# A graph layer on one Trainium2 core: a destination block normalized in its own turn and recorded in three turns instead of six

## The chip, the cores and the metric

The kernel runs on one NeuronCore of a Trainium2 chip. The metric is device time in microseconds (us). Each engine of the core (TensorE or PE, VectorE or DVE, ScalarE or ACT, GpSimd or POOL, SyncE or SP) runs its own stream of instructions in order and waits for the others through semaphores. SP, ACT and POOL also issue DMA transfers; where a profile writes SPq or ACTq it means what those engines' sequencers do, DMA issues above all.

## The reference, cut to what matters

Two graph layers over 100,000 nodes with 64 features and 50,000 edges, each behind a layer norm with a residual. The change touches the second one alone:

```
h = jnp.maximum(_layernorm(x, axis=-1), 0.0)          # x: 100000 x 64, after the first layer
agg = jax.ops.segment_sum(h[src], dst, num_segments=100000)
x = x + relu(agg @ W.T + b)
```

`src` and `dst` are the ends of the 50,000 edges, and `dst` comes sorted. The kernel norms and multiplies a row for every edge (50,000 rows), not for every node, and then sums the results of the edges that share a destination.

## The kernel before, in words

After a stretch of sorting and index arithmetic (up to about 200 us) come two pipelines of the same build, the source side (first layer, to about 888 us) and the **destination side** (second layer, from about 892 us to the end). Each has 98 blocks (BLOCKS) of 512 edges. All that follows is the destination side.

What happens to block b:

- POOL gathers 4 x 128 rows of the node table into a ring of eight buffers `xa` (`gather_x`, L589). Gather b waits until block b - 8 has been normalized (`h_ok`).
- DVE takes mean and variance (`moments`, L1214 and L1219), ACT the root (`deviation`, L746), DVE the reciprocal and the product with the mean (`norm`, L1226 and L1228), ACT the four normalizing activations (`normalize`, L754: `hn`).
- PE transposes `hn` (`turn_h`, L1478: `p_g`), ACT copies that to SBUF (`take_turned`, L762: `agg`), PE multiplies by the weights (`conv`, L1486: `p_m` or `p_z`).
- The result is split into three bf16 parts, a *record*: ACT casts the upper part (`upper`, L700), DVE subtracts it (`remainder`, L1132: `rest`), ACT copies the key and the middle part (`middle`, L705 and L706), DVE subtracts again (`lower`, L1136). ACT stores the record to DRAM (`store_rec`, L712).
- Once block m + 2 is stored, eight *windows* of 112 records are read back for output block m: four by SP (`windows`, L392), four by ACT (`upper_windows`, L680, with their start rows loaded by L673).
- DVE makes one-hot matrices from the keys (`relative`, L1142, and `onehots`, L1158), PE sums the edges of each node with 24 matmuls (`expand`, L1441), and DVE adds the dense block of the node table (`add_dense`, L1180: `dout`). SP loads and stores the dense rows for two blocks at a time (`load_dense`, L402, and `store_dense`, L406, 512 KB each).

Nothing but written code sets the order. Each engine has a loop over *turns* n. In turn n it works on several blocks, each as many turns behind n as a constant says (DST_TAKE, DST_CONV, ...; L57), in the order in which the loop's body names the steps. A step deeper in the pipeline has a larger constant. The loops are ACT's at L766, DVE's at L1231 and PE's at L1490. SP's loop (L428, DST_WIN, DST_HOT and DST_PUT) has turns too; POOL's has none, it goes as far as the ring lets it. Rings of the other buffers: four for records, four for windows, two for `hn`, `agg` and the one-hots, three for the results of `conv` and of `expand`.

## Time and profile before

| what | value |
|---|---|
| median of 3 runs | 1639.02 us (1634.59 to 1651.61) |
| the profiled execution | 1635.77 us, span 1633.9 us |
| source side ends, destination side starts | last `dout` of it at 887.44 us, first gather at 892.61 us |
| destination side, first eight turns | 892.61 to about 978 us |
| turns with gathers | up to 1542.4 us, when the last gather is issued |
| last `sd` (block 97) | 1579.10 us |

A *turn* of ACT is best measured from one `sd` (L746) to the next, since there is one for each block. Times in a timeline count from the span's start. ACT, DVE and PE instructions overlap at their ends: the next one starts before the last is done, so that start to start is the right measure of what one costs on its engine. A register or branch instruction is not counted as busy, but the chain of waits does show it, under ACTq or SPq.

### The profile page before, as it was taken

How to read it: one execution, taken by the hardware profiler on the slowest of the kernel's cores; microseconds unless marked ns; L12 is line 12 of the kernel's file. 1: busy time of each engine (PE TensorE's matmuls, PEld its weight loads, DVE VectorE, ACT ScalarE, POOL GpSimd, SP SyncE). 2: the span in 40 equal slices, each digit the busy share in tenths (PEclk: the TensorE clock that was granted, in tenths of full speed). 3: DMA queues.
4: the chain of work that ended last, by engine and by line, in shares of the span. 5: the costliest groups of instructions: out<-in, count | busy, mean ns of one | idle time of the engine just before them, and what ended most of it. 6: DMA issues, size and time to landing. Idle time of an engine off the chain costs nothing.

```text
span 1633.9 us, 28928 instructions
## 1 busy us (share of the span) xinstructions
PE 892.6 (55%) x8466; PEld 637.4 (39%) x8466; DVE 1005.1 (62%) x2752; ACT 551.4 (34%) x1724; POOL 835.5 (51%) x863
## 2 busy tenths in 40 slices
PE   0120146888887888787894113444545454455553
PEld 0010023555655556555563112333333333333442
DVE  9899955777777877778794113444444444444543
ACT  0300133444444444444451223333333434333430
POOL 4733175666666666666601755555555555555400
PEclk9985555899899998999997555555555555555555
DMA  1000012677777877778787115777787777787789
GB/s 42 0 0 0 15 39 60 166 213 209 205 197 210 230 207 209 203 210 229 207 245 205 27 35 129 168 183 176 167 186 178 181 177 168 171 199 177 177 211 206
DMA packets 486482, 253.92 MB, mean 155 GB/s; under 512 B 417656, under 2 KB 449372, under 8 KB 486322
## 3 DMA queue, kind: packets, MB, share of 16 engines
q1 hardware_dynamic: 376066, 157.65, 39.8%
q10 hardware_dynamic: 85168, 75.08, 15.7%
q0 software_dynamic: 25088, 19.32, 6.4%
q8 instruction: 69, 1.13, 0.3%
q14 instruction: 91, 0.75, 0.2%
HBM read 159.45 MB, written 92.43 MB: 154 GB/s over the span
## 4 chain that ended last, share of the span: by engine, by line
ACT 21%; ACTq 19%; another core or an unknown queue 19%; issue 16%; DVE 14%; PE 6%; DMA 3%; SPq 2%; POOL 1%; DVEq 0%; POOLq 0%
ACTq L680 10%; ACT hn L754 6%; ACT xa L665 4%; ACTq L712 4%; ACTq L686 3%; ACT hid L693 3%; ACT rec L706 3%; ACTq L673 2%; DVE kb L975 2%; DVE ka L975 2%; DVE ka L976 2%; ACT rec L700 2%; DVE kb L976 1%; ACT agg L762 1%
## 5 line engine op out<-in xcount | busy, mean ns | idle before, releaser
L589 POOL DMA_INDIRECT xa<-node_table,gi x392 | 369.8, 943 | 358.1 <-ACT hn L754 159.1
L577 POOL DMA_INDIRECT xa<-in_edge_attr_dram,gi x392 | 390.3, 996 | 278.2 <-issue 94.4
L754 ACT ACTIVATE hn<-xa,nmr,rstd 128x64 f32<-128x64 f32 x392 | 140.4, 428 | 362.8 <-issue 257.8
L1226 DVE RECIPROCAL rstd<-sd 128x4 f32<-128x4 f32 x98 | 17.4, 178 | 322.1 <-ACT sd L746 226.2
L1478 PE MATMUL p_g<-ident,hn 128*128 128x128 f32 x196 | 66.8, 441 | 169.5 <-ACT hn L754 114.4
L700 ACT CAST rec<-p_m 128x256 bf16<-128x256 f32 x164 | 60.5, 369 | 287.0 <-remote 276.4
L1123 DVE TENSOR_TENSOR_SCAN feats<-c_rows,feats,p_g 64x512 f32<-64x512 f32 x97 | 122.7, 1265 | 13.1 <-remote 9.2
L1125 DVE TENSOR_TENSOR_SCAN feats<-c_rows,feats,p_g 32x512 f32<-32x512 f32 x97 | 123.3, 1271 | 1.4
L693 ACT ACTIVATE hid<-p_z,bias_z 128x512 f32<-128x512 f32 x98 | 112.8, 1151 | 32.4 <-issue 16.5
L1418 PE MATMUL p_z<-feats,w_s 96*128 96x512 f32 x196 | 122.1, 709 | 0.1
L1426 PE MATMUL p_m<-w_s,hid 128*128 128x64 f32 x784 | 121.3, 304 | 0.0
L1426 PEld LDWEIGHTS p_m<-w_s,hid 128*128 128x128 f32 x784 | 106.7, 211 | 12.3 <-issue 1.3
L1478 PEld LDWEIGHTS p_g<-ident,hn 128*128 128x128 f32 x196 | 30.2, 205 | 194.4 <-ACT hn L754 131.5
L665 ACT ACTIVATE xa<-xa,share 128x32 f32<-128x32 f32 x392 | 91.7, 307 | 41.3 <-issue 41.1
L1132 DVE TENSOR_TENSOR rest<-p_m,rec 128x256 f32<-128x256 f32 x164 | 68.5, 418 | 50.0 <-ACT rec L700 35.0
L1486 PE MATMUL p_m<-wd,agg 128*128 128x128 f32 x264 | 80.0, 453 | 28.8 <-issue 18.2
L1441 PE MATMUL p_u<-win,oneh 128*128 128x64 bf16 x792 | 54.0, 239 | 69.3 <-issue 42.3
L1441 PE MATMUL p_z<-win,oneh 128*128 128x64 bf16 x768 | 53.4, 238 | 66.1 <-issue 45.3
L1441 PE MATMUL p_t<-win,oneh 128*128 128x64 bf16 x792 | 54.5, 238 | 60.4 <-issue 42.5
L1136 DVE TENSOR_TENSOR rec<-rest 128x256 bf16<-128x256 f32 x196 | 82.8, 423 | 3.5
L1449 PE MATMUL p_t<-win,oneh 128*128 128x64 bf16 x1764 | 70.4, 197 | 23.3 <-issue 18.8
L1449 PEld LDWEIGHTS p_t<-win,oneh 128*128 128x128 bf16 x1764 | 64.6, 101 | 42.3 <-issue 26.6
(281 smaller groups left out, 1827.6 us busy)
## 6 DMA issues: line engine op xcount, KB each, us to landing
records<-rec ACTq DMA_DIRECT2D x196, 196.0 KB
win<-records SPq DMA_DIRECT2D x392, 85.8 KB
node_table<-dout SPq DMA_DIRECT2D x49, 512.0 KB
din<-node_table SPq DMA_DIRECT2D x49, 512.0 KB
out_dram<-dout SPq DMA_DIRECT2D x49, 512.0 KB
din<-in_x_dram SPq DMA_DIRECT2D x48, 512.0 KB
c_rows<-rows_src ACTq DMA_DIRECT2D x141, 128.0 KB
win<-records SPq DMA_DIRECT2D x392, 42.9 KB
```

The lines of the kernel that those rows point to most:

```text
L577: g.indirect_dma_start(out=xa[n % XRING][:, t, 0:FE], out_offset=None, in_=edge_attr, in_offset=bass.IndirectOffsetOnAxis(ap=gi[0][:, BT * ...
L589: g.indirect_dma_start(out=xa[k % XRING][:, t, :], out_offset=None, in_=T, in_offset=bass.IndirectOffsetOnAxis(ap=gi[1][:, BT * n + t:BT * ...
L665: last = s.activation(xa[n % XRING][:, t, FE:2 * FE], xa[n % XRING][:, t, 0:FE], ACT.Copy, scale=share[:, BT * n + t:BT * n + t + 1])
L680: s.dma_start(win[g % WRING][0:WP, PER // 2 + q, :], recs[1][bass.ds(at[q], WP), :]).then_inc(win_in[g % WRING], 16)
L693: s.activation(hid[n % 2][:, :].rearrange("p (t n) -> p n t", n=P), p_z[n % 2][:, :].rearrange("p (n t) -> p n t", t=BT), ACT.Relu, bias=b ...
L754: last = s.activation(hn[n % 2][:, t, :], xa[k % XRING][:, t, :], ACT.Relu, bias=nmr[n % 2][:, t:t + 1], scale=rstd[n % 2][:, t:t + 1])
L1123: v.tensor_tensor_scan(f[0:64, :], c[0:64, at:at + BLK], p_g[n % 2][0:64, :], first[0:64], ALU.mult, ALU.add)
L1125: v.tensor_tensor_scan(f[64:96, :], c[64:96, at:at + BLK], p_g[n % 2][0:32, :], first[64:96], ALU.min, ALU.max).then_inc(feats_ok, 1)
L1418: mm(p_z[n % 2][:, :], w1_s[:, :], feats[n % 2][:, :], start=True, stop=True).then_inc(z_ok, 1)
L1426: last = mm(p_m[n % 2][:, D * t:D * (t + 1)], hid[n % 2][:, P * t:P * (t + 1)], w2_s[:, :], start=False, stop=t == BT - 1)
L1441: last = mm(to[:, D * s:D * (s + 1)], oneh[1][m % HRING][:, s, :], win_words[k % WRING][:, s, D * w:D * (w + 1)], start=w == 0, stop=w == 2)
L1449: last = mm(to[:, (2 * q + t) * D:(2 * q + t + 1) * D], oneh[side][m % HRING][:, q, s, :], win_words[k % WRING][:, 2 * q + a, D * w:D * (w ...
```

## The change

The constants of the destination side shrink: the copy of the transposed block, its convolution and the cast of the upper part stand one turn behind n (they stood two, three and four), the rest of the record two (five), the windows five (nine), one-hots seven (eleven), expansion eight (twelve), the sum nine (thirteen), the store of the sum eleven (fifteen). ACT's loop normalizes block n in turn n, behind `deviation(n)`, with `take_turned(n - 1)` ahead of both; it normalized n - 1 in turn n, ahead of `deviation(n)`. DVE's loop has `norm(n)` ahead of `remainder`. PE's loop goes `conv(n - 1)`, `expand`, `turn_h(n)`; it went `expand`, `conv(n - 3)`, `turn_h(n - 1)`. No instruction, tile, ring or transfer is added or taken away.

```diff
-DST_TAKE, DST_CONV, DST_UP, DST_REC, DST_WIN, DST_HOT, DST_EXP, DST_ADD, DST_PUT = 2, 3, 4, 5, 9, 11, 12, 13, 15
+DST_TAKE, DST_CONV, DST_UP, DST_REC, DST_WIN, DST_HOT, DST_EXP, DST_ADD, DST_PUT = 1, 1, 1, 2, 5, 7, 8, 9, 11
@@ ACT
                 for n in range(BLOCKS + DST_WIN):
-                    if valid(n - 1):
-                        normalize(n - 1)
+                    if valid(n - DST_TAKE):
+                        take_turned(n - DST_TAKE)
                     if valid(n):
                         deviation(n)
-                    if valid(n - DST_TAKE):
-                        take_turned(n - DST_TAKE)
+                    if valid(n):
+                        normalize(n)
                     if valid(n - DST_UP):
                         upper(BLOCKS + n - DST_UP)
@@ DVE
                     if valid(n - DST_HOT):
                         relative(1, n - DST_HOT)
+                    if valid(n):
+                        norm(n)
                     if valid(n - DST_REC):
                         remainder(BLOCKS + n - DST_REC)
-                    if valid(n):
-                        norm(n)
                     if valid(n - DST_REC):
                         lower(BLOCKS + n - DST_REC)
@@ PE
                 for n in range(BLOCKS + DST_EXP):
+                    if valid(n - DST_CONV):
+                        conv(n - DST_CONV)
                     if valid(n - DST_EXP):
                         expand(1, n - DST_EXP)
-                    if valid(n - DST_CONV):
-                        conv(n - DST_CONV)
-                    if valid(n - 1):
-                        turn_h(n - 1)
+                    if valid(n):
+                        turn_h(n)
```

On ACT, in the middle of the destination side, the order of instructions before was this (`xN` is N alike in a row; the register instructions before a window's DMA read ISA; the last two rows come four times in all):

```order
L754 ACTIVATE hn<-xa,nmr,rstd 128x64 x4
L746 ACTIVATE sd<-mv,eps_t 128x4
L762 COPY agg<-p_g 128x256
L700 CAST rec<-p_m 128x4x64
L705 COPY rec<-rn 128x4
L706 COPY rec<-rest 128x4x64
L712 DMA records<-rec 128x392
L673 TENSOR_LOAD start_row
L680 ISA
L680 DMA win<-records 112x98
```

And it is now:

```order
L762 COPY agg<-p_g 128x256
L746 ACTIVATE sd<-mv,eps_t 128x4
L754 ACTIVATE hn<-xa,nmr,rstd 128x64 x4
L700 CAST rec<-p_m 128x4x64
L705 COPY rec<-rn 128x4
L706 COPY rec<-rest 128x4x64
L712 DMA records<-rec 128x392
L673 TENSOR_LOAD start_row
L680 ISA
L680 DMA win<-records 112x98
```

The four `hn` have moved from ahead of `sd` to right behind it, and they are now those of the same block as that `sd`; the copy to `agg` went ahead of it.

On DVE, at the same place, before:

```order
L1214 BN_STATS stat<-xa 128x6 x4
L1219 BN_AGGR mv<-stat 128x2 x4
L1142 TENSOR_TENSOR rel<-win,base_f 112x16
L1132 TENSOR_TENSOR rest<-p_m,rec 128x256
L1226 RECIPROCAL rstd<-sd 128x4
L1228 SCALAR_TENSOR_TENSOR nmr<-mv,rstd 128x4
L1136 TENSOR_TENSOR rec<-rest 128x4x64
L1158 TENSOR_TENSOR oneh_0<-node_of,rel 112x1024
L1180 SCALAR_TENSOR_TENSOR dout<-p_z,din 128x512
```

And now:

```order
L1214 BN_STATS stat<-xa 128x6 x4
L1219 BN_AGGR mv<-stat 128x2 x4
L1142 TENSOR_TENSOR rel<-win,base_f 112x16
L1226 RECIPROCAL rstd<-sd 128x4
L1228 SCALAR_TENSOR_TENSOR nmr<-mv,rstd 128x4
L1132 TENSOR_TENSOR rest<-p_m,rec 128x256
L1136 TENSOR_TENSOR rec<-rest 128x4x64
L1158 TENSOR_TENSOR oneh_0<-node_of,rel 112x1024
L1180 SCALAR_TENSOR_TENSOR dout<-p_t,din 128x512
```

The subtraction that makes `rest` went from ahead of the reciprocal to behind the product `nmr`.

On PE, in the middle of the destination side, one turn and the start of the next, before:

```order
L1441 MATMUL p_t<-win,oneh_0 128x64 x24
L1486 MATMUL p_m<-wd,agg 128x128 x2
L1478 MATMUL p_g<-ident,hn 128x128 x2
L1441 MATMUL p_u<-win,oneh_1 128x64 x24
L1486 MATMUL p_m<-wd,agg 128x128 x2
```

And now:

```order
L1486 MATMUL p_m<-wd,agg 128x128 x2
L1441 MATMUL p_z<-win,oneh_0 128x64 x24
L1478 MATMUL p_g<-ident,hn 128x128 x2
L1486 MATMUL p_m<-wd,agg 128x128 x2
L1441 MATMUL p_t<-win,oneh_1 128x64 x24
```

The convolution stands ahead of the 24 matmuls of the expansion, and the transposes of `hn` behind them, as before.

## Rows read from the trace of the kernel before

**Rows 1.** The profile's page: the chain that ended last, shares of the span by engine

```profile
ACT 21%; ACTq 19%; another core or an unknown queue 19%; issue 16%; DVE 14%; PE 6%; DMA 3%; SPq 2%; POOL 1%; DVEq 0%; POOLq 0%
```

**Rows 2.** Windows: three stretches; busy us per engine, clock share, DMA share, GB/s

```profile
1030.00:1538.00 508.00, 251.58 (x2235) 190.99 (x2235) 234.76 (x1109) 188.65 (x665) 279.02 (x296) 0.51 0.77 177
1538.00:1580.00 42.00, 22.67 (x212) 17.61 (x212) 22.68 (x108) 19.02 (x70) 3.78 (x4) 0.50 0.89 206
1580.00:1634.00 54.00, 20.37 (x302) 18.45 (x302) 22.20 (x48) 5.74 (x21) 0.00 (x0) 0.53 0.92 211
```

**Rows 3.** Tile sd, 1030 to 1538 us, then 1538 to 1580: durations, first and last start

```profile
L746 ACT ACTIVATE sd<-mv,eps_t x73: 281/282/283, 1041.8 to 1531.7; 128x4 f32<-128x4 f32 x73
...
L746 ACT ACTIVATE sd<-mv,eps_t x8: 281/282/283, 1538.3 to 1579.1; 128x4 f32<-128x4 f32 x8
```

**Rows 4.** Timeline of a short turn: start, length, engine, line, idle before and releaser

```profile
1213.16 0.28 ACT L746 ACTIVATE sd<-mv,eps_t 128x4 f32<-128x4 f32 x1
1213.35 0.35 ACT L762 COPY agg<-p_g 128x256 f32<-128x256 f32 x1
1213.47 0.18 DVE L1226 RECIPROCAL rstd<-sd 128x4 f32<-128x4 f32 x1 [5.00 <-ACT sd L746]
1213.68 0.16 DVE L1228 SCALAR_TENSOR_TENSOR nmr<-mv,rstd 128x4 f32<-128x4 f32 x1
1214.93 1.44 PE L1441 MATMUL p_u<-win,oneh 128*128 128x64 bf16 x24 [0.94 <-issue]
1215.34 1.76 ACTq L680 DMA_DIRECT2D win<-records  x4
1216.18 1.20 PE L1486 MATMUL p_m<-wd,agg 128*128 128x128 f32 x4
1216.23 0.14 DVE L1142 TENSOR_TENSOR rel<-win,base_f 112x16 bf16<-112x16 f32 x1
1217.20 1.43 ACT L754 ACTIVATE hn<-xa,nmr,rstd 128x64 f32<-128x64 f32 x4 [2.84 <-issue]
1218.54 0.28 ACT L746 ACTIVATE sd<-mv,eps_t 128x4 f32<-128x4 f32 x1
1218.69 0.69 PE L1478 MATMUL p_g<-ident,hn 128*128 128x128 f32 x2 [1.31 <-issue]
```

**Rows 5.** Timeline of the second turn of the side, ACT otherwise idle

```profile
904.92 0.30 ACT L746 ACTIVATE sd<-mv,eps_t 128x4 f32<-128x4 f32 x1 [2.91 <-DVE mv L1219]
...
905.46 0.16 DVE L1228 SCALAR_TENSOR_TENSOR nmr<-mv,rstd 128x4 f32<-128x4 f32 x1
905.66 1.43 ACT L754 ACTIVATE hn<-xa,nmr,rstd 128x64 f32<-128x64 f32 x4 [0.44 <-DVE nmr L1228]
```

**Rows 6.** Timeline of the long turn before that of rows 4

```profile
1204.93 0.28 ACT L746 ACTIVATE sd<-mv,eps_t 128x4 f32<-128x4 f32 x1
...
1205.29 0.94 POOL L589 DMA_INDIRECT xa<-node_table,gi  x1 [0.77 <-issue]
...
1207.00 0.01 SPq L402 DMA_DIRECT2D din<-node_table  x1
...
1207.13 4.58 ACTq L680 DMA_DIRECT2D win<-records  x4
...
1209.04 0.94 POOL L589 DMA_INDIRECT xa<-node_table,gi  x1 [0.30 <-issue]
```

**Rows 7.** Timeline: DVE's sums, that of block 84 and that of block 97

```profile
1580.64 0.68 DVE L1180 SCALAR_TENSOR_TENSOR dout<-p_t,din 128x512 f32<-128x512 f32 x1
...
1626.99 0.68 DVE L1180 SCALAR_TENSOR_TENSOR dout<-p_u,din 128x512 f32<-128x512 f32 x1
```

**Rows 8.** DMA issues of the whole span: count, KB each, us from issue to landing

```profile
records<-pad_rec SPq DMA_DIRECT2D x2, 196.0 KB, 2.4
```

**Rows 9.** Line 589, 1500 to 1634 us: POOL's gathers, shortest, median and longest in ns

```profile
L589 POOL DMA_INDIRECT xa<-node_table,gi x28: 938/944/947, 1499.3 to 1542.4; - x28
```

**Rows 10.** Lines and tiles, 1100 to 1580 us: the copy to agg, and its waits

```profile
L762 ACT COPY agg<-p_g 128x256 f32<-128x256 f32 x72 | 25.2, 350 | 21.4 <-remote 12.1 <-issue 4.8 <-PE p_g L1478 4.5
```

## The prediction

> **What bounds the kernel now.** I read the page's chain first, then the time by stretch, then one turn in order of time. The chain that ended last runs mostly over ACT and its sequencer, 21% and 19% of the span, more than DVE's 14% and PE's 6% [rows 1]. The change touches the destination side alone, so I cut that into stretches [rows 2]: from 1030 to 1538 us ACT is busy 188.65 of 508 us, PE 251.58, POOL 279.02, the DMA engines 0.77. No engine is full, so a chain of waits or what isn't counted as busy must set the pace. A short turn [rows 4] shows it on ACT: root at 1213.16, the copy and casts behind it, four window transfers issued from 1215.34 to 1217.10, then the four normalizing activations from 1217.20 and the next root at 1218.54. That is 5.38 us with no gap that anybody else ends: "issue" before `hn` covers ACT's own register and DMA-issuing instructions. DVE is through with everything that ACT needs at 1216.23 + 0.14 = 1216.37 and then waits for that root; PE's 24 expansion matmuls and convolution end at 1217.38. **ACT's own list of instructions sets the short turn.**
>
> The mean turn is longer: 72 turns from 1041.8 to 1531.7 are 6.80 us each [rows 3]. The turn before the short one took 1213.16 - 1204.93 = 8.23 us [rows 6]: the same four window issues lasted 4.58 us in place of 1.76. They began 0.13 us after SP had issued the dense load of two blocks, while POOL was issuing gathers (1205.29 to 1209.98). Once the gathers are over the mean falls to (1579.1 - 1538.3) / 7 = 5.83 us [rows 3], with the DMA engines busier (0.89) than before [rows 2]. So ACT's issues are slow where dense transfers and gathers meet, which costs 6.80 - 5.38 = 1.42 us per turn on average, and full DMA engines alone don't explain it.
>
> **The change, part by part.**
>
> *Normalized in its turn.* `normalize(n)` now follows `deviation(n)` directly. It needs DVE's reciprocal and product of the same block, which need that root, and ACT has nothing between. The handoff shows in the second turn of the side, where ACT normalized at once for want of other work: root at 904.92, product at 905.46, `hn` at 905.66, 0.74 us from root to `hn` [rows 5]. In the old order the instruction behind the root started 0.19 us after it (1213.16 to 1213.35) [rows 4]. **The exposed part is 0.55 us a turn.** DVE is idle when the root comes (it was ready 1218.54 - 1216.37 = 2.17 us early), and the reciprocal now goes ahead of the subtraction, so it doesn't grow. Everything else on ACT is as many instructions as before. The first eight turns (to about 978 us) are paced by gathers landing and by something that holds DVE and ACT alike, and I count nothing for them. For the 90 turns of blocks 8 to 97 that is 90 x 0.55 = +49.5 us. Bounds: 0, if the slow stretches swallow it, and 90 x 0.74 = 67 us, if the root's own 0.19 us were to be paid again.
>
> *Four turns fewer to drain.* When the last root is taken (1579.10 us), blocks 84 to 97 still have to be summed; afterwards it is 88 to 97. From the sum of block 84 (1580.64) to that of 97 (1626.99) there are 13 steps of 3.57 us [rows 7], with the DMA engines at 0.92 [rows 2]. Four steps fewer are **-14.3 us**. At most it is four thirteenths of all that comes after the last root, 4 x 54.8 / 13 = 16.9 us; at least 0, if the windows and dense rows that are no longer there return in the turns before.
>
> *Records read back one turn after their store, not two.* The wait in both window steps stands in front of ACT's next copy, root and `hn`, so it would be paid in full. The same amount of records, 196 KB, landed 2.4 us after its issue on an otherwise light chip [rows 8]. Between a store and the wait for it there is at least one whole turn, 5.38 + 0.55 = 5.93 us. Cost 0; it would be something from a landing of 5.9 us on. SP's window issues wait for the same stores and for nothing else that has moved closer: expansion, sums and dense transfers keep their distances to the windows (2 and 4 turns), in SP's queue too.
>
> *Convolution ahead of expansions.* PE's turn becomes a loop with ACT's: copy 0.35, convolution 1.20, expansion 1.44, transposes 0.69 [rows 4], 3.68 us against a turn of 5.93. It leaves 2.2 us; before, the copy took a block transposed a whole turn earlier. Cost 0 in a turn in which PE runs as here. The copy's waits of 21.4 us in 480 [rows 10] say that PE is late now and then already, and it may be more often.
>
> *The subtraction behind the product.* DVE's `rest` comes some 0.3 us later relative to the root, while ACT is at `hn` for 1.43 us. Cost 0. The Trainium skill (Advanced Engine Details and Errata, GPSIMD Details) says that POOL shares a read and a write interface with DVE and conflicts with DVE instructions of two SBUF inputs. By it gathers would be held beside `lower` and the one-hots, and moving them to another part of DVE's turn would matter. Rows speak against it here: 28 gathers took 938 to 947 ns [rows 9], so none was held, and the sum has no term for it.
>
> **Sum:** 1635.8 (the profiled execution) + 49.5 - 14.3 = 1671.0 us. The median of the runs is 3.2 us above that execution. I forecast between the two, **1672 us**, 2% slower.
>
> **Rivals.**
>
> *A, the forecast: ACT pays the handoff in each turn, the drain gives back a third of it.* 1672 us, chance 0.47. Its own range is 1657 to 1694: 70 x 0.55 - 16.9 = +22 at the low end, the upper bound of the handoff with a drain worth 8 us, 67 - 8 = +59, at the high one.
>
> *B, the handoff is hidden and the drain is the whole effect.* The 1.42 us by which the mean turn exceeds ACT's own 5.38 is a cushion if the pace of two turns is set by what gathers and dense rows together allow, and not by ACT's count of instructions. For: a short and a long neighbour make 5.38 + 8.23 = 13.61, just two mean turns. Against: with gathers gone the pace is 5.83 at a higher DMA share, and POOL is busy 55% only [rows 2]. Then 1635.8 - 14.3 = 1621.5 us; if convolution ahead of expansion also removes the copy's waits (21.4 us) [rows 10], 1600. It decides from the point where a turn's slow stretch shrinks by 0.16 us or more for each handoff (14.3 / 90): below that the drain is eaten up. Chance 0.20. With the handoff half hidden it is 1635.8 + 24.7 - 14.3 = 1646 us, no measurable change, chance 0.13; I give it that much because the first eight turns, 85 us for eight blocks, are where I understand the pace least.
>
> *C, the slow stretch grows.* POOL starts a block's gathers when `hn` is done. That was 0.36 us after the root [rows 6] and becomes 0.74 + 1.43 = 2.2 us after it, and the four gathers then run to 6.9 us, beyond the end of a 5.9 us turn. If a slow stretch lasts while gathers and dense rows meet, it lasts up to 1.8 us longer in each of 45 pairs of turns, 81 us; half of it gives 1672 + 40 = 1712 us. PE's smaller cushion works the same way. For: the long turn's slow issues end just after the last gather. Against: the dense rows' own time isn't longer. Chance 0.18.
>
> *D, the wait for records.* If landings are at 7 us under load, 1 us in each turn is added, 1762 us. Chance 0.02.
>
> **Numbers.** The range takes in A, most of C and B down to its drain-only figure: 1616 to 1714 us. What a measurement of this kernel can tell from no change is about 1%, so 1623 to 1655 is the same. Slower by more: A, C and D, 0.47 + 0.18 + 0.02 = 0.67. Within: the half-hidden handoff, 0.13. Faster: B, 0.20.
>
> **What would show it.** In the changed profile, from root to `hn` 0.74 us in every turn, with DVE's product as what ended ACT's wait; short turns of 5.9 us; a mean turn of 7.3 to 7.4 from 1030 us on; nine sums left after the turn of the last root, which stands 38 to 41 us before the end; transfers of records never waited for. B would show a mean turn of 6.8 or less with the same 0.74 in it. C would show a mean of 7.8 and more, with window issues of 4 us and longer in more turns than now. A's gain is wrong if the last nine sums take as long as thirteen did. The forecast as a whole is wrong if ACT's turn isn't what bounds: if short turns stay at 5.4 us, or if ACT waits for PE's transposes.

## The result, and the profile after

| | before | after |
|---|---|---|
| median of the runs | 1637.76 us (1634.59 to 1651.61, 4 runs) | 1658.14 us (1653.46 to 1660.81, 4 runs) |
| span of the profiled execution | 1633.9 us | 1658.9 us |

The ratio is 1.0102, 95% interval 1.0065 to 1.0139: 1% slower, 20 us. I had forecast 1672 us, 34 us more than the median above. The difference of the two profiled executions, 25.0 us, splits as follows (a turn is timed from `sd` to `sd`):

| us | first `sd` at | blocks 0 to 8 | blocks 8 to 97 (mean turn) | last `sd` to the end |
|---|---|---|---|---|
| before | 899.8 | 78.4 | 600.8 (6.75) | 54.8 |
| after | 903.9 | 82.4 | 630.5 (7.08) | 42.0 |
| difference | +4.1 | +4.0 | +29.7 | -12.8 |

The first column is the source side, which the change doesn't touch. The drain came out near the forecast (-14.3). Of +49.5 us in the turns only 29.7 are there.

One profile used below, `a0`, is of an execution that took 1781 us, 330 us more than the other runs of that kernel; nearly all of it lies ahead of the destination side, TensorE's expansion matmuls are recorded there with 293 ns instead of 242, and its turns (587.1 us) agree with those of `e8` (588.4), the same kernel but for one move on DVE.

The chain that ended last on the page after answers to [rows 1]; "another core or an unknown queue" has grown from 19 to 23%:

```profile
another core or an unknown queue 23%; ACT 18%; ACTq 17%; issue 17%; DVE 16%; PE 4%; DMA 2%; SPq 2%; POOL 1%; DVEq 0%; POOLq 0%
```

Stretches of the destination side after, in the columns of [rows 2]: with gathers, then the drain.

```profile
1035.00:1535.00 500.00, 206.24 (x2100) 173.11 (x2100) 228.45 (x1050) 186.00 (x630) 263.50 (x281) 0.55 0.70 170
...
1617.00:1659.00 42.00, 14.33 (x226) 12.92 (x226) 15.40 (x33) 3.91 (x14) 0.00 (x0) 0.55 0.84 192
```

PE is less busy (0.41 of the stretch, before 0.50), POOL a little less (0.53, before 0.55), ACT as much as before (0.37), and the DMA engines fell from 0.77 to 0.70. The turns by `sd` answer to [rows 3], (1529.8 - 1035.2) / 69 = 7.17 us each in this stretch:

```profile
L746 ACT ACTIVATE sd<-mv,eps_t x70: 299/300/301, 1035.2 to 1529.8; 128x4 f32<-128x4 f32 x70
```

The timeline after, a long turn and the short one behind it (lines left out in between), answers to [rows 4, 6]:

```profile
1205.54 0.30 ACT L746 ACTIVATE sd<-mv,eps_t 128x4 f32<-128x4 f32 x1
1206.28 1.43 ACT L754 ACTIVATE hn<-xa,nmr,rstd 128x64 f32<-128x64 f32 x4 [0.44 <-issue]
1206.71 1.49 PE L1441 MATMUL p_u<-win,oneh 128*128 128x64 bf16 x24
1207.98 0.94 POOL L589 DMA_INDIRECT xa<-node_table,gi  x1 [1.25 <-ACT hn L754]
1208.02 0.67 PE L1478 MATMUL p_g<-ident,hn 128*128 128x128 f32 x2
1208.17 0.42 SPq L402 DMA_DIRECT2D din<-node_table  x1
1208.65 1.66 SPq L406 DMA_DIRECT2D out_dram<-dout  x1
1209.45 1.97 ACTq L680 DMA_DIRECT2D win<-records  x4
1211.73 0.94 POOL L589 DMA_INDIRECT xa<-node_table,gi  x1 [0.31 <-issue]
1213.84 0.37 ACT L762 COPY agg<-p_g 128x256 f32<-128x256 f32 x1 [5.47 <-remote]
1214.11 0.30 ACT L746 ACTIVATE sd<-mv,eps_t 128x4 f32<-128x4 f32 x1
1214.86 1.43 ACT L754 ACTIVATE hn<-xa,nmr,rstd 128x64 f32<-128x64 f32 x4 [0.44 <-DVE nmr L1228]
...
1220.06 0.30 ACT L746 ACTIVATE sd<-mv,eps_t 128x4 f32<-128x4 f32 x1
```

The short turn is 5.95 us (forecast 5.93), and root to `hn` is 0.74 us in each turn. The long one is the puzzle. ACT is through with its window issues at 1211.42, PE's transposes ended at 1208.69 by their record, and yet the copy of `p_g` starts at 1213.84. "Remote" means that the profile finds nobody who was done just then. ACT waited 2.42 us there. The profile's row for the copy shows more, since ACT's idle time before it now takes in ACT's own record and window issues, some 2.8 us in every turn:

```profile
L762 ACT COPY agg<-p_g 128x256 f32<-128x256 f32 x68 | 25.3, 372 | 273.8 <-remote 140.4 <-issue 133.5
```

Counted from the end of ACT's last issue, 26 of these 68 copies waited, 56 us in all, 2.7 us at most. In [rows 10] it was 21.4 us on four copies of 72.

Behind the last root (1616.9 us) ten sums are left, those of blocks 88 to 97, as forecast: that of block 88 in the same turn and nine behind it. Before, there were fourteen. They are slower per step, (1652.26 - 1618.90) / 9 = 3.71 us against 3.57 in [rows 7]:

```profile
1618.90 0.69 DVE L1180 SCALAR_TENSOR_TENSOR dout<-p_u,din 128x512 f32<-128x512 f32 x1
...
1652.26 0.68 DVE L1180 SCALAR_TENSOR_TENSOR dout<-p_u,din 128x512 f32<-128x512 f32 x1
```

A gather takes what it took in [rows 9]:

```profile
L589 POOL DMA_INDIRECT xa<-node_table,gi x40: 939/943/947, 1503.4 to 1570.6; - x40
```

### The profile page after: what moved, and what is told of

It is laid out like the page before. It is cut to its first block, busy times and chain, and to the rows that moved or that the text cites. A ratio compares the mean times of both kernels' runs of the same rounds, so it can differ in the third digit from the quotient of the medians.

```text
span 1658.9 us, 28928 instructions
## 1 busy us (share of the span) xinstructions
PE 847.8 (51%) x8466; PEld 628.3 (38%) x8466; DVE 1013.3 (61%) x2752; ACT 560.1 (34%) x1724; POOL 837.5 (50%) x863
## 4 chain that ended last, share of the span: by engine, by line
another core or an unknown queue 23%; ACT 18%; ACTq 17%; issue 17%; DVE 16%; PE 4%; DMA 2%; SPq 2%; POOL 1%; DVEq 0%; POOLq 0%
ACTq L680 8%; ACT xa L665 5%; ACT hn L754 4%; ACTq L712 4%; ACTq L686 3%; ACT hid L693 3%; ACT rec L706 3%; DVE kb L975 2%; DVE ka L975 2%; ACTq L673 2%; DVE ka L976 2%; DVE kb L976 1%; ACT sd L746 1%; ACT rec L700 1%
## 5 line engine op out<-in xcount | busy, mean ns | idle before, releaser
L1486 PEld LDWEIGHTS p_m<-wd,agg 128*128 128x128 f32 x264 | 58.6, 309 | 283.2 <-ACT agg L762 164.1
L762 ACT COPY agg<-p_g 128x256 f32<-128x256 f32 x98 | 36.5, 372 | 376.3 <-issue 200.1
L1418 PE MATMUL p_z<-feats,w_s 96*128 96x512 f32 x196 | 118.4, 689 | 2.5 <-issue 2.5
L1486 PE MATMUL p_z<-wd,agg 128*128 128x128 f32 x128 | 37.9, 449 | 134.1 <-ACT agg L762 81.8
L665 ACT ACTIVATE xa<-xa,share 128x32 f32<-128x32 f32 x392 | 91.7, 307 | 39.8 <-issue 39.6
L1449 PE MATMUL p_t<-win,oneh 128*128 128x64 bf16 x1764 | 74.8, 201 | 20.1 <-issue 16.0
L1486 PEld LDWEIGHTS p_z<-wd,agg 128*128 128x128 f32 x128 | 28.6, 311 | 147.0 <-ACT agg L762 87.8
L1449 PEld LDWEIGHTS p_t<-win,oneh 128*128 128x128 bf16 x1764 | 68.6, 104 | 40.3 <-issue 24.5
## 6 DMA issues: line engine op xcount, KB each, us to landing
win<-records SPq DMA_DIRECT2D x392, 42.9 KB
```

The lines of the kernel that those rows point to most:

```text
L665: last = s.activation(xa[n % XRING][:, t, FE:2 * FE], xa[n % XRING][:, t, 0:FE], ACT.Copy, scale=share[:, BT * n + t:BT * n + t + 1])
L1418: mm(p_z[n % 2][:, :], w1_s[:, :], feats[n % 2][:, :], start=True, stop=True).then_inc(z_ok, 1)
L1449: last = mm(to[:, (2 * q + t) * D:(2 * q + t + 1) * D], oneh[side][m % HRING][:, q, s, :], win_words[k % WRING][:, 2 * q + a, D * w:D * (w ...
L1486: last = mm(p_d[1][n % 3][:, P * h:P * (h + 1)], agg[n % 2][:, P * h:P * (h + 1)], wd[:, :, :].rearrange("p t d -> p (t d)"), start=True, ...
```

## Two kinds of chips, and TensorE's held increments

The first eight experiments and two of the last fell on chips on which the kernel before takes 1387 to 1389 us; eight others on chips where it takes 1626 to 1636, near the 1638 of the result. Each is compared with the kernel before on its own chip. The changed kernel is 4.7% slower on the first kind (`a0`) and 1.2% on the second (`a1`). TensorE's granted clock doesn't tell them apart: 0.51 over blocks 8 to 97 on the slower chip, 0.50 on the faster (before, b0), both the lower of its two levels, 1.2 GHz, for nearly all of the time. What differs shows first in the trace's list of semaphore events. For the long turn above (times in us; the increments belong to the last matmul of each group):

```
group            recorded end   increment seen   who starts on it
expansion p_u    1208.20        1213.78          SP's next window issues, 1213.80
transposes p_g   1208.68        1213.82          ACT's copy to agg, 1213.84
last gather of POOL's train of four ended at 1212.67
```

Both increments come 5.1 to 5.6 us late, together, and 1.1 us behind POOL's last gather. PE was not working: they are 0.04 us apart, the groups' recorded ends 0.48. The Trainium skill (TensorE: Matmul & The Clock Gate, The cost: per-tile semaphore tail) puts increments on completion at some 26 ns each, one after another. Where nothing is held the trace shows 0.01 us behind the recorded end, as little as that; holds of microseconds aren't in it.

I call an increment **held** when it is seen over 0.5 us behind its matmul's recorded end, and count those of convolution, expansion and transposes between the roots of blocks 12 and 88, 228 in each run, wherever the trace has the event (the first of that semaphore behind the matmul's end and ahead of the end of the next group of its kind):

| run | chip | increments | held |
|---|---|---|---|
| before | slower | 186 | 116 |
| after (again: a1) | slower | 133 (132) | 63 (66) |
| e11 before_shorter | slower | 194 | 107 |
| e10, before with 2 KB pieces | slower | 176 | 112 |
| e9, after with 2 KB pieces | slower | 121 | 51 |
| e12 after_gather_late | slower | 155 | 46 (mean of these under 1 us) |
| e7 after_far | slower | 122 | 0 |
| e13 and e14, one gather | slower | 155, 190 | 0, 0 |
| b0, a0, e1 to e6, e8, e15 | faster | 192 to 227 each | 0 |

By the place in POOL's train of four gathers (4.7 us long), on the slower chips: 2 to 4 us into a train 80 of 83 increments were held (before). In the first microsecond, after: 58 of 65 where SP's dense load had been issued within the 1.5 us before or 0.6 us behind, and 0 of 23 elsewhere. The load's place isn't the rule in general, though: in the first microsecond in before 22 of 31 were held with no dense load that near. More than 6 us behind a train's start, so over 1.3 us behind its end: 2 of 55 (before), 0 of 38 (after). 49 of the 63 releases in after came 1.06 to 1.17 us behind the last gather's end, 91 of the 116 in before 1.2 to 1.7 us; in e9, and for half of those of e11, they came elsewhere.

In the kernel before more than increments is slow. On the timeline right behind [rows 4] (lines left out in between) PE crawls:

```profile
1220.32 1.01 PE L1441 MATMUL p_z<-win,oneh 128*128 128x64 bf16 x16 [0.94 <-DVE oneh L1158]
...
1222.65 0.94 POOL L589 DMA_INDIRECT xa<-node_table,gi  x1 [0.30 <-issue]
1222.85 0.21 PE L1441 MATMUL p_z<-win,oneh 128*128 128x64 bf16 x1 [1.52 <-issue]
1224.28 0.21 PE L1441 MATMUL p_z<-win,oneh 128*128 128x64 bf16 x1 [1.22 <-issue]
1225.02 0.48 PE L1441 MATMUL p_z<-win,oneh 128*128 128x64 bf16 x6 [0.53 <-issue]
...
1225.57 0.77 ACT L754 ACTIVATE hn<-xa,nmr,rstd 128x64 f32<-128x64 f32 x2 [5.82 <-PE p_z L1441]
```

The increments of expansion, convolution and transposes from 1216.37 on were seen at 1225.16, 1225.22 and 1225.26, within 0.1 us of each other. But a held increment doesn't explain the crawl itself: the 24 matmuls of an expansion wait for nothing in between, and PE still stood between them. From start to start it took over 0.4 us 120 times between blocks 12 and 88, 1.0 us on average. ACT does the same in that kernel. The 4.58 us of its four window issues in [rows 6] are steps of 0.70 to 0.72 us, register instructions that wait for nothing and take 0.03 us elsewhere (shortest, median and longest in ns, 1100 to 1580 us):

```profile
L680 ACTq FUSED_REGOPS  x284: 3/37/724, 1103.3 to 1577.2; - x142
```

Register instructions of over 0.3 us, of some 608 on each engine between blocks 12 and 88: before 38 on ACT and 57 on SP; after none on ACT (37 ns each) and 40 on SP; e7 none and 34; e13 and e14, with one gather, none at all, and none in any of the ten traces from faster chips. So the trains slow several engines there, and held increments are one form of it. Whether both have one cause stays open.

## The experiments

Distances are given in the order TAKE, CONV, UP, REC, WIN, HOT, EXP, ADD, PUT. "Main" is the time from block 8's `sd` to block 97's in the profiled execution.

| run | ratio to before | 95% interval | first eight | main (mean turn) | drain |
|---|---|---|---|---|---|
| faster chips: b0 before | 1.0009 | 0.9989 to 1.0029 | 40.0 | 514.3 (5.78) | 54.2 |
| a0 after | 1.0472 | 1.0442 to 1.0503 | 43.1 | 587.1 (6.60) | 41.9 |
| e1 after_pe_old | 1.0518 | 1.0482 to 1.0554 | 43.0 | 594.6 (6.68) | 41.8 |
| e2 before_pe_new | 0.9983 | 0.9963 to 1.0003 | 40.0 | 515.8 (5.80) | 54.8 |
| e3 four_turns | 1.0149 | 1.0108 to 1.0189 | 41.2 | 545.1 (6.12) | 46.0 |
| e4 after_long_tail | 1.0327 | 1.0289 to 1.0365 | 41.2 | 554.1 (6.23) | 57.0 |
| e5 handoff_only | 1.0516 | 1.0490 to 1.0542 | 39.9 | 582.0 (6.54) | 56.6 |
| e6 four_turns_far | 1.0107 | 1.0087 to 1.0127 | 41.0 | 535.9 (6.02) | 47.4 |
| e8 after_dve_old | 1.0463 | 1.0435 to 1.0490 | 42.9 | 588.4 (6.61) | 43.3 |
| e15 = e7 | 1.0242 | 1.0213 to 1.0271 | 42.3 | 554.4 (6.23) | 42.0 |
| slower chips: a1 after | 1.0115 | 1.0082 to 1.0149 | 82.2 | 630.0 (7.08) | 43.1 |
| e7 after_far | 0.9746 | 0.9709 to 0.9782 | 81.7 | 562.0 (6.31) | 43.7 |
| e9 after_2kb | 0.9880 | 0.9843 to 0.9917 | 81.4 | 590.4 (6.63) | 39.6 |
| e10 before_2kb | 1.0043 | 1.0004 to 1.0083 | 78.3 | 612.4 (6.88) | 51.4 |
| e11 before_shorter | 1.0340 | 1.0294 to 1.0386 | 78.9 | 648.3 (7.28) | 52.6 |
| e12 after_gather_late | 0.9852 | 0.9819 to 0.9884 | 81.5 | 582.2 (6.54) | 42.4 |
| e13 before_one_gather | 0.9087 | 0.9061 to 0.9114 | 22.7 | 509.0 (5.72) | 54.6 |
| e14 after_one_gather | 0.9566 | 0.9538 to 0.9594 | 35.1 | 584.4 (6.57) | 42.7 |

(The destination side of a0's profile is 63.6 us longer than that of b0; the medians differ by 64 us.)

### PE's order alone: e2 and e1

e2 is the kernel before with

```diff
-                    if valid(n - DST_EXP):
-                        expand(1, n - DST_EXP)
                     if valid(n - DST_CONV):
                         conv(n - DST_CONV)
+                    if valid(n - DST_EXP):
+                        expand(1, n - DST_EXP)
```

> The kernel before with PE's new order alone: convolution (still of block n - 3) ahead of expansion. Theory 1 (PE's place): the 20 us by which the handoff cost less than forecast are the turns of 10 us and more that the kernel before has (six of them between blocks 8 and 97, together 20 us over 8.23 us each) and the changed one has not; they come from PE's 24 expansion matmuls standing ahead of convolution and transposes while SP's dense transfers are under way. Then 1638 - 20 = 1618 us, and no turn over 9.5 us. Theory 2 (the gathers' place): the 20 us are a part of the handoff that ran beside slow stretches, PE's order has nothing to do with it: 1638 us, and the turns of 10 us stay.

e1 is the changed kernel with the opposite edit.

> The changed kernel with PE's old order: expansion ahead of convolution (all turns as in the changed kernel). Theory 1: expansion now starts right behind the transposes, at the moment at which SP issues the dense transfers, so the long turns come back: 1658 + 20 = 1678 us or more, with turns of 10 us and above. Theory 2: 1658 us, turns of 5.9 and 8.6 us in alternation as in the changed kernel.

e2 did nothing (0.9983), e1 cost 7.5 us in the main stretch. Where nothing is held the move is worth 0 in the kernel before and 7.5 us in the changed one. Neither run fell on a slower chip, the only kind that shows turns of 10 us, so the theory that the order hides 20 us wasn't tested where it would have to hold.

### The distances: e3, e4, e6

e3 is the kernel before with PE's new order, distances 2, 2, 2, 3, 6, 8, 9, 10, 12 and `take_turned(n - 2)` ahead of `normalize(n - 1)`, so without the handoff:

```diff
+                    if valid(n - DST_TAKE):
+                        take_turned(n - DST_TAKE)
                     if valid(n - 1):
                         normalize(n - 1)
                     if valid(n):
                         deviation(n)
-                    if valid(n - DST_TAKE):
-                        take_turned(n - DST_TAKE)
```

> A schedule without the handoff: ACT goes take_turned(n - 2), normalize(n - 1), deviation(n), upper(n - 2); PE convolution(n - 2), expansion, transposes(n - 1); DVE as before; constants 2, 2, 2, 3, 6, 8, 9, 10, 12, so that a record takes four turns. Theory 1: short turns of 5.4 us, no turn over 9.5 us, three turns fewer to drain: 1638 - 20 - 3 x 3.57 = 1607 us. Theory 2: the handoff's real price was (29.7 us over 90 turns) 0.33 us, so 1658 - 30 + 3.6 = 1632 us.

e4 is the changed kernel with the old distances from the windows on:

```diff
-... = 1, 1, 1, 2, 5, 7, 8, 9, 11
+... = 1, 1, 1, 2, 9, 11, 12, 13, 15
```

> The changed kernel with the later half of the pipeline as deep as before: windows, one-hots, expansion, sum and store at 9, 11, 12, 13, 15 turns. If the four turns fewer to drain are worth what the end of the two profiles shows (54.8 us against 42.0 us after the last root), it is 1658 + 12.8 = 1671 us. If what the drain saves comes back in the turns before, since the same transfers then run there, it is 1658 us.

e6 is e3 with distances 2, 2, 2, 3, 7, 9, 10, 11, 13.

> The four-turn schedule without the handoff (1410 us, ratio 1.015) with its windows one turn later (constants 2, 2, 2, 3, 7, 9, 10, 11, 13), so that a record is read back two turns after its store, as in the kernel before. Theory 4 (records): what made the four-turn schedule slower than the kernel before is that SP waits for the landing of a record stored one turn earlier (134.8 us of waits in 400 us), and so issues the dense transfers when ACT issues its windows. Then the mean turn is 5.80 us again and two turns less have to be drained: 1389 - 7 = 1382 us, ratio 0.995. If the records' distance has no part in it, it is 1410 + 3.6 = 1413 us, ratio 1.017.

e4's main stretch is 33 us shorter than a0's although ACT's order is the same; its longer drain gives 15 back. e3 has no handoff and still lost 31 us in its turns. So something in the distances isn't free. e6 was to show that it is the records, with turns of 5.80 us and a ratio of 0.995. It missed: SP waits for no record there (e3: 134.8 us, 62 times, 900 to 1300 us), ACT's four window issues take 1.97 us (e3: 2.38), but the turns fell by 9 us only, of e3's 31. The other 22 us of that schedule stay open.

### The handoff alone: e5, and the controls b0 and a0

e5 is the kernel before with `take_turned(n - 2)`, `deviation(n)`, `normalize(n)` on ACT; nothing else.

> The kernel before with ACT normalizing block n in turn n behind deviation(n), and nothing else changed (copy to agg of n - 2 still ahead of both, all depths, DVE's and PE's order as before). Theory 3: 90 turns x 0.55 us = +49.5 us, 1438 us, ratio 1.036, short turns 5.9 us. Theory 2: +30 us, ratio 1.021.

> The kernel before, unchanged, for its trace under the conditions in which the experiments run, where it takes 1389 us and not 1638: by both theories as its own runs, ratio 1.00. If the 10 us turns and the eight slow first turns of the first profile are a property of that chip's conditions, they are missing here.

> The changed kernel, unchanged, under the same conditions. Theory 3: the forecast's terms hold (handoff +49.5 us, drain -14.3 us), and the 20 us that were missing from the handoff in the first pair of profiles are the long turns of the kernel before, which exist only under the conditions of that pair. Then 1389 + 35 = 1424 us, ratio 1.025. Theory 2 (the slow stretches swallow a part of the handoff everywhere): ratio 1.01, 1405 us.

e5 costs 67.7 us in its turns, more than the 49.5 of the handoff. ACT's window issues are longer too: 2.44 us for the four of a turn, mean of blocks 20 to 88 (a0 2.42, b0 2.12, e4 2.00, e6 1.97). These 0.32 us over b0 are 28 us in 89 turns and leave 39 for the handoff. They depend on how long ago SP issued its dense load. On the timeline of a0 the four last 3.02 us when they start 2.9 us behind it and 1.77 us when 10 us behind:

```profile
1311.28 1.77 ACTq L680 DMA_DIRECT2D win<-records  x4
1313.41 0.30 ACT L746 ACTIVATE sd<-mv,eps_t 128x4 f32<-128x4 f32 x1
1314.35 0.42 SPq L402 DMA_DIRECT2D din<-node_table  x1
1314.82 1.83 SPq L406 DMA_DIRECT2D out_dram<-dout  x1
1317.22 3.02 ACTq L680 DMA_DIRECT2D win<-records  x4
```

And SP issues the dense load late because its queue waited for records. SP's own waits in a0, 1230 to 1630 us (total, times, longest):

```profile
SPq L392 <- DMA records<-rec: 160.2, 60, 5.6
```

In e5 it is 123.7 us, 60 times (900 to 1300 us), though records are read back two turns after their store there, and 27.0 us, 34 times, in b0. So two turns are not always enough: the distance and the order of the engines decide it together.

### Records read back two turns after their store: e7 and e15

The changed kernel with windows and all behind them one turn deeper:

```diff
-... = 1, 1, 1, 2, 5, 7, 8, 9, 11
+... = 1, 1, 1, 2, 6, 8, 9, 10, 12
```

> The changed kernel with windows, one-hots, expansion, sum and store one turn deeper (6, 8, 9, 10, 12), so that records are read back two turns after their store, as before. Theory 1 (SP waits for records one turn old, and so issues its dense load where it slows ACT's window issues): the mean turn of blocks 8 to 97 falls from 6.60 us to about 6.3, ratio to before 1.02 to 1.035 in place of 1.047, drain 42 to 46 us. Theory 2 (the handoff of 0.55 us and ACT's late window issues are the whole of it, wherever the records stand): mean turn 6.6, ratio 1.047 to 1.052 (one more turn to drain, +3 us).

> The changed kernel with windows, one-hots, expansion, sum and store one turn deeper, once more. Theory H (TensorE's increments are held by gathers on some chips): on a chip that holds, 0.975 as measured; on one that doesn't, the kernel before has nothing to lose there, the handoff is paid, and the ratio is 1.03 to 1.04 (mean turn 6.2 to 6.3 against 5.8, drain 10 us shorter). Rival P (dense transfers' phase alone): 0.975 on every chip.

On the faster chip (e15) SP no longer waits for records at all; it waits for the windows' ring (900 to 1300 us):

```profile
SPq L386 <- PE p_t L1441: 52.2, 22, 3.7
SPq L386 <- PE p_z L1441: 51.6, 21, 4.0
SPq L386 <- PE p_u L1441: 49.8, 21, 3.7
```

Its turns are 32.7 us shorter than a0's, in all (window issues 1.95 us). On the slower chip (e7) it is 2.5% faster than the kernel before. No increment between blocks 12 and 88 is held, and the turns take 562.0 us, near the 554.4 of the faster chip. The chip is one that holds: three convolutions of e7's own first eight turns were seen 6.2 us late. Its timeline:

```profile
1206.18 0.30 ACT L746 ACTIVATE sd<-mv,eps_t 128x4 f32<-128x4 f32 x1
1206.92 1.43 ACT L754 ACTIVATE hn<-xa,nmr,rstd 128x64 f32<-128x64 f32 x4 [0.44 <-issue]
1208.62 0.95 POOL L589 DMA_INDIRECT xa<-node_table,gi  x1 [1.64 <-ACT hn L754]
1208.65 0.67 PE L1478 MATMUL p_g<-ident,hn 128*128 128x128 f32 x2
1210.02 1.82 ACTq L680 DMA_DIRECT2D win<-records  x4
1211.42 0.34 SPq L402 DMA_DIRECT2D din<-node_table  x1
1211.94 0.37 ACT L762 COPY agg<-p_g 128x256 f32<-128x256 f32 x1 [2.92 <-issue]
1212.21 0.30 ACT L746 ACTIVATE sd<-mv,eps_t 128x4 f32<-128x4 f32 x1
```

It is the long turn of the kernel after up to the transposes, but the dense load goes out 2.8 us behind the train's start, not 0.19 us, and the transposes' increment was seen at 1209.33, at once.

### The dense pieces: e9 and e10

The destination side's dense rows in the source side's layout, 2 KB pieces instead of 256 bytes, in the changed kernel (e9) and in that before (e10). The same bytes move, but dense rows meet the sums of other nodes, so a part of the computation is another one:

```diff
         def rows_of(table, side, k):
...
-            if side == 0:
+            if True:
...
         def pair_rows(tile, side):
-            if side == 0:
+            if True:
```

> The changed kernel with the destination side's dense rows loaded and stored in the layout of the source side: 2 KB pieces in place of 256 bytes, the same bytes. Changed part of the computation: the dense rows meet the expansion's sums of other nodes, so the output isn't the reference's. Theory 1 (a window issue is slow while the queue's hardware is busy with the many small pieces of the dense load): ACT's four window issues fall from 2.42 us to about 1.8, the mean turn from 6.60 to 6.0 or less, main stretch at least 27 us shorter, ratio to before 1.02 or less. Theory 2 (issues are slow for another reason, the number of bytes in flight or ACT's own waits): span of the four issues 2.4 and mean turn 6.6 as without the edit, ratio 1.045.

> The kernel before with the same edit of the dense layout (again only a part of the computation is another one: dense rows meet the wrong nodes), as the control. Theory 1: before's dense issue falls together with ACT's own window issues, which cost 2.12 us a turn in place of about 1.8, so 0.2 to 0.3 us a turn is gained, 20 to 30 us, ratio 0.98 to 0.985, and the changed kernel with the edit stands 1.02 to 1.03 above this one (handoff less drain, +36 us of about 1365). Theory 2: no change, ratio 1.00.

Theory 1 missed in both. Theory 2 has e10's ratio and e9's mean turn (6.63) and issues (2.36 us), but not e9's ratio: it took 1.045, that of the faster chips. The window issues were not made faster by large pieces: on e9's timeline the four still take 2.99 us, 1 us behind the dense load.

```profile
1227.54 0.40 SPq L402 DMA_DIRECT2D din<-node_table  x1
1228.00 0.45 SPq L406 DMA_DIRECT2D out_dram<-dout  x1
1228.54 2.99 ACTq L680 DMA_DIRECT2D win<-records  x4
1231.63 0.37 ACT L762 COPY agg<-p_g 128x256 f32<-128x256 f32 x1 [4.10 <-issue]
```

So the small pieces are not what slows an issue. e9's gain, 40 us against after (on another slower chip), goes with shorter holds: 51 of 121 held, and for those of transposes the mean over all is 1.5 us, after 2.8. SP's issue of the dense store itself fell from 1.66 to 0.45 us. e10 (1.0043) gained nothing.

### A shorter pipeline in ACT's old order: e11

The kernel before with PE's new order and distances 2, 2, 3, 4, 8, 10, 11, 12, 14, meant to beat both.

> The kernel before with only the distances cut where nothing has to wait for it: convolution ahead of expansion on PE and two turns behind n, upper part three, rest of the record four, windows eight, one-hots ten, expansion eleven, sum twelve, store fourteen; ACT's and DVE's order as before, records still read back two turns after their store and more. One turn less to drain (-3.5 us) and no handoff. Theory: mean turn 5.78 as before, ratio 0.997. Rival: the shorter distance on PE, or windows in another phase to the dense load, costs more than the drain gives: ratio 1.00 to 1.01.

It lost 3.4%. The chip was a slower one, and 83 of 84 increments that fell 2 to 4 us into a train were held there. This sent me to the semaphore events.

### Gathers as the cause: a1, e12, e13, e14

a1 is the changed kernel again. e12 starts the gathers behind the transposes:

```diff
-                    pool.wait_ge(h_ok, n - XRING + 1)
+                    pool.wait_ge(ht_ok, n - XRING + 1)
```

e13 (before) and e14 (after) issue one gather of four on the destination side, and DVE waits for as many; three quarters of the rows are left out of the computation:

```diff
-                for t in range(BT):
+                for t in range(1):
                     g.indirect_dma_start(
...
-                    dve.wait_ge(gathered[k % XRING], 16 * BT * (k // XRING + 1))
+                    dve.wait_ge(gathered[k % XRING], 16 * (k // XRING + 1 + (BT - 1) * len(range(k % XRING, BLOCKS, XRING))))
```

> The changed kernel as it is, timed beside the one with windows one turn later. Theory H (on some chips an increment of a semaphore by TensorE that falls more than about 1.3 us into a train of gathers is held until 1.1 us behind the train's end; there both kernels take over 1600 us, on chips without it 1390 and 1450): if this chip holds, ratio about 1.01, and increments held 4 to 9 us in both kernels; if it doesn't, ratio 1.047 and no increment later than 0.1 us. Rival P (it is the phase of dense transfers and window issues alone, on every chip): ratio the same, 1.01 or 1.047, with no relation to what TensorE's increments do.

> The changed kernel, but POOL starts a block's gathers once TensorE has transposed the block eight before it, 0.7 us later than when that was normalized. All three increments of TensorE's turn then come before the train. Theory H: on a chip that holds, no increment is held, the turns of 8.5 us go and the mean turn of blocks 8 to 97 falls from 7.08 to 6.3 or less, 70 us, ratio to before about 0.97; on a chip that doesn't hold, no change against the changed kernel (1.047). Rival P: no change on any chip, since dense transfers and windows stand where they stood.

> The kernel before, with one of a block's four gathers on the destination side; three quarters of its rows are left out of the computation (what the buffer held stands in their place). Theory H: trains of one gather hold nothing, so on a chip that holds the mean turn of blocks 8 to 97 falls from 6.7 us to ACT's own 5.4 to 5.8, at least 90 us, and the first eight turns from 78 us to 40 or less, ratio 0.92 or less; on a chip that doesn't hold it stays at 5.8, ratio 0.98 to 1.00. Rival P: windows and dense transfers are as before, so 6.5 or more on a chip of over 1600 us.

> The changed kernel with the same three gathers in four left out. Theory H: without holds the changed kernel is slower than the one before with the same edit by the handoff less the drain, 0.55 x 90 - 12 = 37 us and more where windows are issued behind a dense load (up to 65): mean turn 6.0 to 6.6, on either kind of chip. Rival P: the difference between the two kernels stays as small as it was measured first, 20 to 25 us, on a chip of over 1600 us.

The chip was a slower one. With one gather no increment was held and no register instruction was slow, and the turns are those of the faster chips: 5.72 us against 5.78 before, 6.57 against 6.60 after. e12 took 48 us out of the turns, of the 70 expected, by a start 0.7 us later (POOL's wait is now for `p_g`); that no increment would be held missed: 46 of 155 were, by 1 us, most of them of expansions that fall on a train's end. POOL's wait in e12, 1035 to 1480 us (total, times, longest):

```profile
POOL xa L589 <- PE p_g L1478: 121.2, 68, 2.6
```

The rival, that dense transfers and window issues alone set it, fell: neither was touched.

### DVE's order alone: e8

The changed kernel with `remainder` ahead of `norm` again.

> The changed kernel with DVE's old order alone: the subtraction that makes rest ahead of reciprocal and product. The prediction's cost of that move was 0. Theory: the subtraction has all it needs before the root comes, 1 us or more, so from root to hn it stays 0.74 us and the ratio to before is that of the changed kernel within 0.5%, 1.047 or 1.01 according to the chip. Rival: the subtraction is late and stands in the root's way, root to hn 0.9 to 1.1 us and 15 to 30 us more in all.

Root to `hn` stayed at 0.74 us, the ratio at 1.0463. The move costs nothing.

## Why the prediction was wrong

Against the forecast's steps:

1. **"Normalized in its turn", +49.5 us: right in its mechanism and about right in size.** 0.74 us in each turn, short turns of 5.95 us. With the dense load out of the way (e15) the turns cost 40.1 us more than before, with window issues 0.17 us shorter than b0's; e5 leaves 39 us once its longer issues are taken off. No run has the handoff with everything else as it was.
2. **"Four turns fewer to drain", -14.3 us: right, a little large.** -12.8 measured, -12.3 and -11.9 in the other two pairs.
3. **Records read back one turn after their store, "cost 0": the step that failed.** I asked only whether a landing outlasts a turn in front of ACT's work, and took its length from a light stretch [rows 8]. But SP's queue waited for records, 2.7 us in each turn of a0, and its dense load stands behind those waits. On the slower chip too: between its wait for the expansion and the first window that needs the record SP stood 95 us in 47 of 76 turns (after), and never in before or e7. (The profile's list of waits names 1.6 us of it, since that trace lacks most landings of records.) That put the load 3 us ahead of ACT's window issues instead of beside or far from them, 33 us in all on the faster chips (a0 against e15). On the slower ones it put it into the first microsecond of POOL's train, beside TensorE's increments: 58 of 65 held. One turn more there is worth 630.5 - 562.0 = 68.5 us (two slower chips). Why the load's place matters to the increments isn't shown, only that it does in this kernel.
4. **"ACT's issues are slow where dense transfers and gathers meet", 1.42 us a turn, left unchanged: failed too, the other way.** The observation was right as far as it went; to let it stand unchanged was the error. Of the 1.42 us, (600.8 - 509.0) / 89 = 1.03 us end with the trains of gathers (e13). Some 0.45 of them are ACT's own window issues, 2.58 us in before and 2.13 in e13; the rest goes with TensorE's held increments, which I hadn't seen. The changed kernel has 630.5 - 584.4 = 46.1 us of such time instead of 91.8. Its window issues are no longer slowed (2.10 us; 2.35 in e14), and all of a turn's PE work now ends within a microsecond of the train's start, not in its middle: 63 increments held instead of 116. That is where the expected loss went.

The sum for the turns: with one gather the change costs 584.4 - 509.0 = 75.4 us (72.8 on the faster chips), that is the forecast's 49.5 for the handoff and 25.9 for the rest, which I put down to step 3 (e15 has 40.1 and 32.7 for the two); what the trains cost falls by 91.8 - 46.1 = 45.7; together 29.7. Two errors of opposite sign, 26 and 46 us, left the turns 20 us under the forecast. That they nearly met was luck. (The last sum uses executions on more than one slower chip.)

5. **Convolution ahead of expansions, cost 0:** right in the kernel before where nothing is held (e2); in the changed kernel the new order saves 7.5 us there (e1). On slower chips it wasn't tested alone: e11, which has it, lost, but with other distances too.
6. **Subtraction behind the product, cost 0:** right (e8).
7. **The first eight turns, nothing counted:** +4.0 and +3.1 us. Part of what I didn't understand there are holds: POOL gathers without pause, the first three turns are quick, and from the fourth on all seven increments in the trace came 1.2 to 5.0 us late. The turns take up to 17 us, so other waits belong to it that I can't name. They take 78.4 us on the slower chips, 40.0 on the faster, 22.7 with one gather.

Of the rivals, C had the right place (gathers and dense rows meeting) and the wrong sign; B's cushion exists, but in what the trains slow down, and gives back 45.7 of the 75.4 us that the change costs with one gather. D's price was put on ACT; it fell due in SP's queue.

Left open: why some chips hold increments and slow register instructions and others don't, and whether it is POOL's issuing or the gathers' traffic that does it. e13 takes away both, the issuing and the traffic. I took no run that parts them, and none that tells whether the recording of the trace has a part in it: of the 228 increments 95 are missing in after, 36 in b0 and 1 in a0.

The version with windows at distance 6 is faster than both kernels on the slower chips (0.9746) and slower than the one before on the faster (1.0242). Nothing here is shown to beat the kernel before on both: e2 (0.9983, faster chips alone) is no different from it, and e12 (0.9852) ran on a slower chip alone.

## What to carry to other kernels

Where a mean turn is longer than the engine's own list of work, find what fills the rest before adding a term to it: look at when semaphores are seen, not when their instructions ended, and at register instructions that take longer than their fellows. "Remote" waits of two engines that end in the same instant can point to one held signal. When a distance is shortened, price it in every queue that waits for it and ask where the next big transfer in that queue then falls. And compare on more than one chip: a 1% loss here was 4.7% there, and a 2.5% gain a 2.4% loss.

## What the runs showed of the hardware

- On some chips increments by TensorE that fell into a train of indirect gathers were seen up to 10.7 us late (before; 13.3 in e10), in before mostly 1.2 to 1.7 us behind the train's last gather, in after 1.1 us; on others never over 0.1 us, though b0 issues 256 gathers without a longer pause than 0.3 us. Increments of ACT and DVE that fell into the same holds, 143 in before and 75 in after, were not late.
- On the same chips, and only with trains of four gathers, register instructions of SP (57 of 608) and of ACT (38 of 608) took over 0.3 us, mostly 0.70, instead of 0.03, and PE stood between the matmuls of one expansion (before).
- The same program takes 1388 us on one kind and 1637 on the other, with the same durations of single instructions: a gather 0.94 us, `hn` 1.43.
- Four window issues of ACT take 1.8 us far from a dense load of 512 KB and 3.0 to 3.1 us when they start 1.5 to 3 us behind its issue; pieces of 2 KB instead of 256 bytes don't change that.
